# Token rows scattered back tile by tile, expert buffers of their own, and the split of the maxima moved off VectorE

## The chip, the cores and the metric

The kernel runs on one core of one Trainium2 chip, in float32 with some bf16 operands. The metric is the device time of one execution in microseconds (us), the median of several runs. A profile of one execution gives the rows quoted below.

## The reference

Two batches of tokens, each of 1024 rows with 128 features go through two layers. Layer 0 is a retention block (8 heads) and then a latent attention (16 heads of 8, causal) followed by a mixture of four experts, of which each row takes the best one. Layer 1 is a plain attention (16 heads of 8, with two masked corner scores) followed by a ternary linear layer. Cut to what the change touches:

```
logits = x @ gate_w.T + gate_b
top = argmax(logits, -1); onehot = one_hot(top, 4)
h = relu(einsum('btd,ehd->bteh', x, W1) + b1)
y = einsum('bteh,edh->bted', h, W2) + b2
moe = einsum('bted,bte->btd', y, onehot)

scores = where(causal, q @ k.T / sqrt(8), -inf)    # layer 1: no causal mask
attn = softmax(scores); out = (attn @ v) @ Wo.T
```

## The kernel before, in words

The retention comes first, then a short stage that makes queries and keys of the latent attention, and then one long stage, attention(), from some 350 us to the end, in which both attentions, the experts and the last layer are interleaved. All five engines walk through one list that order() (L855) returns; each engine takes from it the items that are its own.

**Units.** The scores are worked through in 32 blocks m (16 of the causal layer, m < BLOCKS, and 16 of layer 1). A block is four heads by 512 queries; its units are key tiles of 128: 4 or 8 per block in the causal layer, 8 in layer 1, 224 in all. Batch 0 of layer 0 is units 0 to 47, batch 1 48 to 95, batch 0 of layer 1 96 to 159, batch 1 of layer 1 160 to 223. The list counts in steps, and step s holds unit s: S (L1190, scores by TensorE), the exponentials by ScalarE (L1358), V (L1220, the product with the values, one unit behind), and one or two scans of a later unit.

**Maxima.** A scan is A (L1159): TensorE computes the scores of a later unit in another layout and VectorE reduces them to maxima (L1441). When a block is scanned, the item M turns 16 rows of 128 maxima into three bf16 parts of the negated maximum, which become extra rows of the queries, so that the softmax needs no subtraction. M is a transpose on TensorE (L1172), two operations on VectorE (L1454 and L1456), two on GpSimd (L1062 and L1063), and three small DMAs which GpSimd issues (L1070). The first S of the block waits for these DMAs. M comes 4 steps before that S in layer 1 (3 in its first block); in the causal layer it comes 3 steps before for blocks of 8 units and 7 for blocks of 4.

**PSUM ring.** Items that need a bank of their own (A, M, O, N, Y, H, G, C, x, h, y, D, k, q, v) share a ring of two places; TensorE fills a place once its reader, VectorE or ScalarE, has emptied it.

**Experts.** experts_of(b) (L834) puts the mixture of batch b into the list, from step z on (55 and 103). Rows are normed; TensorE makes the logits (G) and ranks (C); GpSimd scatters eight tiles of rows with indirect DMAs into an order by expert in DRAM (`sort`, L1083). Each expert's rows begin on a tile, so there are 11 tiles, some with rows that no token fills. SyncE loads them as one transfer (L981). x (L1280) transposes them, in three groups; h (L1295) and y (L1303) are the two products of a tile, with weights picked by a register. VectorE adds the bias and writes y over the row tile (L1546). The tiles come four to a step, from step z + 15 on.

**The way back.** store_rows (L997) on SyncE stores the results to DRAM in three groups. The item `back` on GpSimd (at step 73 for batch 0, and at step 120 for batch 1) waits for these three stores, gathers eight tiles of 128 rows in token order with indirect DMAs (L1093), and writes the constant columns of V again (L1097 and L1098), as the expert buffers of a batch lie in the space of its V. `sum` (L1104, step z + 22) adds them to the rows in two halves, `stat` on VectorE (L1552) takes the statistics of a half, `root` (L1110) is GpSimd's, `scale` (L1560) VectorE's over all eight tiles, and D, k, q, v (L1311, L1316, L1321) make the operands of layer 1. GpSimd's own items stand in one order, so an M that comes behind `back` waits for all of it.

**Weights of the experts.** w2 and b2 lie in the space of the query and key parts, so load_picks_of (L970) loads them for each batch.

## Time and profile before

| | |
|---|---|
| median of 3 runs | 1110.97 us (1110.78 to 1114.72) |
| profiled execution, its own time | 1113.98 us |
| its span | 1112.2 us |
| mean granted clock of TensorE | 0.921 |
| TensorE busy | 927.1 us (83%) |
| VectorE busy | 829.0 us (75%) |
| ScalarE busy | 650.0 us (58%) |
| GpSimd busy | 325.7 us (29%) |

Busy time is a mean over stages that differ: retention up to some 300 us, the causal layer and the experts of batch 0 up to some 650 us, layer 1 with the experts of batch 1 up to some 860 us, and the rest. The granted clock is a share of 2.4 GHz; 0.5 is 1.2 GHz. "Idle before" in square brackets is the time in which the engine had nothing running just before the instruction, with what ended it. TensorE's operand loads are PEld.

### The profile page before, as it was taken

How to read it: one execution, taken by the hardware profiler on the slowest of the kernel's cores; microseconds unless marked ns; L12 is line 12 of the kernel's file. 1: busy time of each engine (PE TensorE's matmuls, PEld its weight loads, DVE VectorE, ACT ScalarE, POOL GpSimd, SP SyncE). 2: the span in 40 equal slices, each digit the busy share in tenths (PEclk: the TensorE clock that was granted, in tenths of full speed). 3: DMA queues.
4: the chain of work that ended last, by engine and by line, in shares of the span. 5: the costliest groups of instructions: out<-in, count | busy, mean ns of one | idle time of the engine just before them, and what ended most of it. 6: DMA issues, size and time to landing. Idle time of an engine off the chain costs nothing.

```text
span 1112.2 us, 22861 instructions
## 1 busy us (share of the span) xinstructions
PE 927.1 (83%) x9022; PEld 479.3 (43%) x9022; DVE 829.0 (75%) x1377; ACT 650.0 (58%) x1311; POOL 325.7 (29%) x556
## 2 busy tenths in 40 slices
PE   5999999984675999989896678888969999999982
PEld 3777778774332344344382322336413223222231
DVE  3666667753857788887755658886778999999865
ACT  1555555453321677776634445865747888898860
POOL 2755566642232111102506200240431100100111
PEclk8999999996765899999998888999988999999995
DMA  7000000000041124301331232023204010000000
GB/s 269 1 2 1 1 1 2 1 1 6 1 154 46 35 75 130 88 24 35 102 87 28 81 108 78 21 58 94 80 4 164 19 35 18 20 18 2 5 20 19
DMA packets 50094, 53.79 MB, mean 48 GB/s; under 512 B 8635, under 2 KB 41147, under 8 KB 49701
## 3 DMA queue, kind: packets, MB, share of 16 engines
q1 hardware_dynamic: 45892, 49.79, 14.8%
q0 software_dynamic: 4096, 2.54, 0.9%
q8 instruction: 72, 1.18, 0.4%
q14 instruction: 34, 0.27, 0.1%
HBM read 33.66 MB, written 19.66 MB: 48 GB/s over the span
## 4 chain that ended last, share of the span: by engine, by line
PE 37%; DVE 26%; POOL 17%; issue 12%; ACT 6%; DMA 1%; SPq 0%; POOLq 0%; DVEq 0%; ACTq 0%
DVE arena L1441 16%; PE banks L1220 11%; PE banks L1190 7%; PE banks L1159 4%; ACT arena L1358 3%; POOL arena L711 2%; PE banks L1303 2%; PE banks L1295 2%; POOL arena L384 2%; POOL arena L710 2%; POOL arena L387 1%; POOL arena L714 1%; POOL arena L695 1%; POOL arena L1093 1%; PE banks L1198 1%
## 5 line engine op out<-in xcount | busy, mean ns | idle before, releaser
L1358 ACT ACTIVATE arena<-banks 128x512 f32<-128x512 f32 (+3 forms) x896 | 445.5, 552 | 181.0 <-PE banks L1198 86.5
L1441 DVE TENSOR_REDUCE arena<-banks 128x2 f32<-128x1024 f32 (+1 forms) x448 | 476.5, 1107 | 57.6 <-PE banks L1166 30.8
L1220 PE MATMUL banks<-arena 128*32 128x256 f32 (+1 forms) x3328 | 266.3, 393 | 10.3 <-ACT arena L1371 8.7
L1190 PE MATMUL banks<-arena 61*128 61x512 bf16 (+4 forms) x896 | 169.6, 374 | 36.4 <-ACT arena L1358 28.3
L1159 PE MATMUL banks<-arena 56*128 56x512 bf16 (+3 forms) x896 | 170.4, 376 | 28.0 <-DVE arena L1441 26.4
L1062 POOL CAST arena<-arena 16x128 bf16<-16x128 f32 x32 | 9.0, 281 | 441.4 <-DVE arena L1456 441.3
L1190 PEld LDWEIGHTS banks<-arena 61*128 61x128 bf16 (+1 forms) x896 | 44.3, 93 | 196.0 <-ACT arena L1358 164.5
L1220 PEld LDWEIGHTS banks<-arena 128*32 128x32 f32 x3328 | 67.2, 109 | 140.0 <-issue 78.9
L1159 PEld LDWEIGHTS banks<-arena 56*128 56x128 bf16 x896 | 45.4, 96 | 49.8 <-DVE arena L1441 45.1
L609 DVE TENSOR_REDUCE arena<-arena 128x8 f32<-128x1024 f32 x16 | 19.5, 1220 | 60.7 <-ACT arena L737 60.7
L734 ACT ACTIVATE arena<-banks 128x1024 f32<-128x1024 f32 x16 | 16.4, 1027 | 71.0 <-PE banks L584 69.3
L1070 POOL DMA_DIRECT2D arena<-arena x96 | 54.7, 574 | 10.7 <-POOL arena L1063 9.2
L748 ACT ACTIVATE arena<-banks,arena 128x128 f32<-128x128 f32 x128 | 46.4, 475 | 4.8 <-PE banks L593 4.8
L1166 PE MATMUL banks<-arena 64*128 64x128 bf16 x576 | 46.3, 232 | 0.0
L569 PE MATMUL banks<-arena 128*128 128x128 f32 x256 | 34.9, 292 | 7.9 <-DVE arena L641 7.9
L760 ACT ACTIVATE arena<-banks 128x1024 f32<-128x1024 f32 x16 | 16.4, 1027 | 37.7 <-PE banks L546 36.3
L1198 PE MATMUL banks<-arena 64*128 64x128 bf16 x512 | 37.4, 224 | 0.0
L569 PEld LDWEIGHTS banks<-arena 128*128 128x128 f32 x256 | 31.9, 202 | 10.6 <-DVE arena L641 8.5
L1166 PEld LDWEIGHTS banks<-arena 64*128 64x128 bf16 x576 | 30.0, 103 | 14.0 <-issue 4.4
L654 DVE TENSOR_TENSOR arena<-arena 128x1024 f32<-128x1024 f32 x16 | 32.9, 2059 | 3.0 <-POOL arena L387 3.0
L508 PE MATMUL banks<-arena 128*128 128x512 f32 x64 | 32.7, 634 | 2.1 <-DMA arena<-c_gk 2.1
L546 PE MATMUL banks<-arena 128*128 128x128 f32 x256 | 33.6, 286 | 0.2 <-DVE arena L623 0.2
(217 smaller groups left out, 1366.8 us busy)
## 6 DMA issues: line engine op xcount, KB each, us to landing
arena<-k_products SPq DMA_DIRECT2D x32, 224.0 KB
arena<-q_products SPq DMA_DIRECT2D x64, 112.0 KB
q_products<-arena SPq DMA_DIRECT2D x16, 384.0 KB, 3.4
k_products<-arena SPq DMA_DIRECT2D x16, 384.0 KB, 3.6
arena<-e_w SPq DMA_DIRECT2D x22, 256.0 KB, 3.8
arena<-e_w SPq DMA_DIRECT2D x2, 1024.0 KB, 6.6
arena<-arena POOLq DMA_DIRECT2D x96, 4.0 KB, 1.7
sorted_rows<-x SPq DMA_DIRECT2D x2, 704.0 KB, 8.6
```

The source lines that it names most:

```text
L546: ins = nc.tensor.matmul(bank(s // 4)[:, (s % 4) * P:(s % 4 + 1) * P], wg[:, s * P:(s + 1) * P], XT[:, i, :], start=True, stop=True)
L569: ins = nc.tensor.matmul(bank(7)[:, 0:P], uu[:, s, :], wo[:, s, :], start=(s == 0), stop=(s == RH - 1))
L654: v_.tensor_tensor(on, oc[i % 2], spread(grs, RH, P), ALU.mult).then_inc(o_normed, 1)
L748: ins = s_.activation(ga[:, s, :], bank(4 + s // 4)[:, (s % 4) * P:(s % 4 + 1) * P], ACT.Identity, scale=gn[:, 0, s:s + 1], bias=gn[:, 1, ...
L1070: g_.dma_start(rows, nmp[k % 2][:, i, :]).then_inc(mrow[k % 2], 16)
L1159: ins = nc.tensor.matmul(bank(first + par)[:, 0:hi - lo], Qs[k_][rows, qc, x, qo:qo + P], Ks[k_][rows, x, lo:hi], start=True, stop=not (di ...
L1166: ins = nc.tensor.matmul(bank(first + par)[:, o:o + P], masks[rows, one, :], masks[rows, two, :], start=False, stop=z == len(terms) - 1)
L1190: ins = nc.tensor.matmul(bank((q + par) % SCORES)[:, o:C], Ks[n % NS][rows, x, kt * P:(kt + 1) * P], Qs[n % NS][rows, c, x, o:C], start=Tr ...
L1198: ins = nc.tensor.matmul(bank((q + par) % SCORES)[:, o:o + P], masks[rows, 2 + z, :], masks[rows, z, :], start=False, stop=z == 1)
L1220: ins = nc.tensor.matmul(PS[h * VW:(h + 1) * VW, AV_BANK, o:end], V[:, b, kt, HG * g + h, :], Pr[u % PROBS][:, h, o:end], start=(kt == 0 a ...
L1358: s_.activation(Pr[s % PROBS][:, h, o:C], bank(q % SCORES)[:, o:C], ACT.Exp) \
L1441: v_.tensor_reduce(of, two_banks, AX.X, ALU.max).then_inc(ring_dve, 1)
```

## The change

1. **Scatter in place of gather.** Every sorted row carries its token number as a 129th column, so a row is 516 bytes. Rows that no token fills get numbers beyond the tokens (c_pads). A new item `put` (b, i), one step after y (b, i), scatters tile i with an indirect DMA to the token's place in DRAM. fetch_rows on SyncE waits for all 11 and loads the rows back with two plain transfers. store_rows and `back` are gone, and so is the writing of V's constant columns inside `back`.
2. **Space of their own** for xs, hsT, hid, hn, yg, b2 and w2, one set for both batches. b2 and w2 are loaded once.
3. **M** is read from PSUM by ScalarE (one operation, which copies with a factor of -1), and GpSimd makes all three parts (four operations). VectorE has no part in it.
4. **Batch 1's experts** come two tiles to a step over six steps in place of three, and `sum` comes at z + 26 in place of z + 22; what follows it moves with it.
5. **scale** is split in two halves one step apart; D of the first half waits only for its own.

```diff
+    pads = np.zeros((SORTED * P, P + 1), dtype=np.uint32)
+    pads[:, P] = T + np.arange(SORTED * P)
+    c["c_pads"] = pads.view(f)
+    c["c_token"] = np.arange(T, dtype=np.uint32).reshape(NT, P).T.copy().view(f)
...
-        xs_dram = [nc.dram_tensor(f"sorted_rows_{b}", [SORTED * P, P], F32, kind="Internal").ap() for b in range(B)]
-        ys_dram = [nc.dram_tensor(f"expert_rows_{b}", [SORTED * P, P], F32, kind="Internal").ap() for b in range(B)]
+        xs_dram = [nc.dram_tensor(f"sorted_rows_{b}", [SORTED * P, P + 1], F32, kind="Internal").ap() for b in range(B)]
+        ys_dram = [nc.dram_tensor(f"expert_rows_{b}", [T + SORTED * P, P], F32, kind="Internal").ap() for b in range(B)]
...
-        value_at = A.at
...
-        nm1 = A.tile(P, rows=MAXIMA)
+        nm1, nm2 = A.tile(P, rows=MAXIMA), A.tile(P, rows=MAXIMA)
...
+        xs, hsT, hid = A.tile(SORTED, P + 1), A.tile(SORTED * P), [A.tile(HID) for _ in range(2)]
+        hn = A.tile(NT, P + 1)
+        yg_at = A.at
+        h2T = A.tile(T)
+        A.at = yg_at
+        yg = A.tile(NT, P)
+        b2, w2, token = A.tile(NE * P), A.tile(NE * EM, P), A.tile(NT)
...
-        b2, w2 = A.tile(NE * P), A.tile(NE * EM, P)
...
-        xs, hsT, hid = [], [], []
-        for b in range(B):
-            A.at = value_at + b * NT * AH * VW
-            xs.append(A.tile(SORTED, P))
-            hsT.append(A.tile(SORTED * P))
-            hid.append([A.tile(HID) for _ in range(2)])
-            assert A.at <= value_at + (b + 1) * NT * AH * VW
...
-                sp.dma_start(xs_dram[b], d["x"][0:SORTED * P, :]).then_inc(xs_cleared, 16)
+                sp.dma_start(xs_dram[b], d["c_pads"]).then_inc(xs_cleared, 16)
...
-        BACK_AT = (18, 17)
...
+            pace, end = ((4, 22), (2, 26))[b]
...
-                  (14, ("x", (b, 0))), (14, ("x", (b, 1))), (15, ("x", (b, 2)))]
...
+            at += [(14 + g * 4 // pace, ("x", (b, g))) for g in range(len(GROUPS))]
             for i in range(SORTED + 1):
-                step = 15 + min(i, SORTED - 1) // 4
+                step = 15 + min(i, SORTED - 1) // pace
...
+                at += [(step + 1, ("put", (b, i - 1)))] * (i > 0)
...
-            at += [(BACK_AT[b], ("back", b)), (22, ("sum", b)), (23, ("stat", (b, 0))), (24, ("stat", (b, 1))),
-                   (24, ("root", b)), (25, ("scale", b)), (26, ("D", one)), (26, ("D", two)),
...
+            at += [(end, ("sum", b)), (end + 1, ("stat", (b, 0))), (end + 2, ("stat", (b, 1))), (end + 2, ("root", b))]
+            at += [(end + 3 + d, e) for d, e in (
+                (0, ("scale", one)), (1, ("scale", two)), (1, ("D", one)), (1, ("D", two)),
+                (1, ("k", one)), (1, ("q", one)), (1, ("k_part0", one)), (1, ("k_rem", one)), (1, ("q_part0", one)),
+                (2, ("k", two)), (2, ("q", two)), (2, ("q_rem", one)), (2, ("k_part1", one)), (2, ("k_part2", one)),
...
-        BY_ACT, BY_BOTH = "H x k".split(), "h"
+        BY_ACT, BY_BOTH = "M H x k".split(), "h"
...
-                    sp.dma_start(xs[b], xs_dram[b].rearrange("(i p) o -> p i o", p=P)).then_inc(xs_loaded[b], 16)
+                    if b:
+                        sp.wait_ge(ys_put[b - 1], 16 * SORTED)
+                    sp.dma_start(xs, xs_dram[b].rearrange("(i p) o -> p i o", p=P)).then_inc(xs_loaded[b], 16)
...
-                def store_rows(b, steer):
-                    back = ys_dram[b].rearrange("(i p) o -> p i o", p=P)
-                    for g in GROUPS:
-                        for i in g:
-                            if i + W1S < SORTED:
-                                load_w1(b, i + W1S, steer)
-                        t = slice(g[0], g[-1] + 1)
-                        taken(sp, "y", (b, g[-1]))
-                        sp.dma_start(back[:, t, :], xs[b][:, t, :]).then_inc(ys_stored[b], 16)
+                def fetch_rows(b):
+
+                    sp.wait_ge(ys_put[b], 16 * SORTED)
+                    sp.wait_ge(x_summed, 2 * b)
+                    rows = ys_dram[b][0:T].rearrange("(t p) o -> p t o", p=P)
+                    for c in range(2):
+                        t = slice(QT * c, QT * (c + 1))
+                        sp.dma_start(yg[:, t, :], rows[:, t, :]).then_inc(ys_back[c], 16)
...
-                    store_rows(b, steer)
+                    for i in range(W1S, SORTED):
+                        load_w1(b, i, steer)
...
+                for t, src in ((gate, d["e_gate"]), (enorm, d["k_norm"]), (w2, d["e_w2"])):
...
+                fetch_rows(0)
...
+                pool.wait_ge(load2, 160)
+                link(g_.tensor_copy(hn[:, :, P].bitcast(U32), token.bitcast(U32)))
...
-                        link(g_.tensor_copy(part[1], nm1))
-                        g_.tensor_tensor(part[2], nm1, part[1], ALU.subtract).then_inc(m_split, 1)
+                        ready(pool, mrow[k % 2], PARTS * 16 * (k // 2))
+                        link(g_.tensor_copy(part[0], nm1))
+                        link(g_.tensor_tensor(nm2, nm1, part[0], ALU.subtract))
+                        link(g_.tensor_copy(part[1], nm2))
+                        g_.tensor_tensor(part[2], nm2, part[1], ALU.subtract).then_inc(m_split, 1)
...
-                    elif kind == "back":
-
-                        pool.wait_ge(ys_stored[k], 16 * len(GROUPS))
-                        for t in range(NT):
-                            g_.indirect_dma_start(yg[:, t, :], None, ys_dram[k],
-                                                  bass.IndirectOffsetOnAxis(slot_i[:, t:t + 1], 0)) \
-                              .then_inc(ys_back[t // QT], 16)
-                        pads = V[:, k, :, :, AD:VW].rearrange("p t h e -> p (t h) e")
-                        g_.memset(pads[:, :, 0:1], 1.0)
-                        g_.memset(pads[:, :, 1:VW - AD], 0.0).then_inc(padded, 1)
+                    elif kind == "put":
+
+                        b, i = k
+                        taken(pool, "y", k)
+                        g_.indirect_dma_start(ys_dram[b], bass.IndirectOffsetOnAxis(xs[:, i, P:].bitcast(U32), 0),
+                                              xs[:, i, 0:P], None).then_inc(ys_put[b], 16)
...
-                            pool.wait_ge(ys_back[c], 16 * QT * (k + 1))
+                            pool.wait_ge(ys_back[c], 16 * (k + 1))
...
-                                    pe.wait_ge(padded, b + 2)
...
-                        pe.wait_ge(x1_ready, k // 2 + 1)
+                        pe.wait_ge(x1_ready, k + 1)
...
+                    elif kind == "M":
...
+                        ready(act, m_split, k)
+                        s_.activation(nm1, bank(ring_bank(r))[0:MAXIMA, 0:P], ACT.Copy, scale=-1.0).then_inc(ring_act, 1)
...
-                    elif kind == "M":
-
-                        ready(dve, mrow[k % 2], PARTS * 16 * (k // 2))
-                        row = bk[0:MAXIMA, 0:P]
-                        part = [nmp[k % 2][:, i, :] for i in range(PARTS)]
-                        link(v_.tensor_scalar(part[0], row, -1.0, None, ALU.mult))
-                        ready(dve, m_split, k)
-                        v_.scalar_tensor_tensor(out=nm1, in0=row, scalar=-1.0, in1=part[0],
-                                                op0=ALU.mult, op1=ALU.subtract).then_inc(ring_dve, 1)
...
-                        dve.wait_ge(x_rooted, k + 1)
-                        for i in range(k * NT, (k + 1) * NT):
+                        dve.wait_ge(x_rooted, k // 2 + 1)
+                        for i in range(k * QT, (k + 1) * QT):
```

## Rows read from the trace of the kernel before

**Rows 1.** Page, busy time and share of the span by engine.
```profile
PE 927.1 (83%) x9022; PEld 479.3 (43%) x9022; DVE 829.0 (75%) x1377; ACT 650.0 (58%) x1311; POOL 325.7 (29%) x556
```
**Rows 2.** Timeline, 589 to 610 us: start, length, engine, line, count, [idle before].
```profile
589.84 1.05 POOL L1093 DMA_INDIRECT arena<-expert_rows,arena  x1 [0.30 <-issue]
...
596.73 0.28 DVE L1456 SCALAR_TENSOR_TENSOR arena<-banks,arena 16x128 f32<-16x128 f32 x1
...
599.83 2.73 POOL L1098 MEMSET arena<- 128x2944 f32 x1
...
606.67 0.87 DVE L1552 BATCH_NORM_STATS2 arena<-arena 128x6 f32<-128x128 f32 x4 [8.22 <-POOL arena L1104]
...
609.11 1.12 PE L1228 MATMUL banks<-arena 128*128 128x128 f32 x4 [8.31 <-DVE arena L1441]
```
**Rows 3.** Windows of 3 us: busy PE, PEld, DVE, ACT, POOL, then clock, DMA.
```profile
609.00:612.00 3.00, 2.89 (x24) 1.56 (x24) 2.82 (x11) 0.92 (x2) 0.00 (x0) 0.50 0.00 0
...
810.00:813.00 3.00, 2.81 (x18) 0.64 (x22) 2.97 (x11) 0.62 (x2) 0.36 (x2) 0.53 0.00 0
```
**Rows 4.** Timeline, 806 to 811 us.
```profile
806.42 2.53 POOL L1104 TENSOR_TENSOR arena<-arena 128x512 f32<-128x512 f32 x2
807.58 0.39 PE L1190 MATMUL banks<-arena 61*128 61x512 bf16 x2 [2.28 <-DMA arena<-arena]
807.74 0.87 DVE L1552 BATCH_NORM_STATS2 arena<-arena 128x6 f32<-128x128 f32 x4 [3.95 <-POOL arena L1104]
...
810.19 0.61 PE L1159 MATMUL banks<-arena 56*128 56x512 bf16 x2 [2.22 <-DVE arena L1441]
```
**Rows 5.** Groups of VectorE by shape, 860 to 1040 us: count, busy, mean ns, idle before.
```profile
L1456 DVE SCALAR_TENSOR_TENSOR arena<-banks,arena 16x128 f32<-16x128 f32 x9 | 2.5, 280 | 0.3
L1454 DVE TENSOR_SCALAR arena<-banks 16x128 bf16<-16x128 f32 x9 | 2.4, 268 | 0.0
```
**Rows 6.** Windows of 20 us: experts of batch 1, then last stage.
```profile
760.00:780.00 20.00, 18.09 (x158) 14.85 (x160) 9.95 (x27) 8.49 (x23) 0.00 (x0) 1.00 0.42 104
...
880.00:900.00 20.00, 19.07 (x205) 5.18 (x201) 19.46 (x22) 17.68 (x35) 2.36 (x5) 1.00 0.09 25
```
**Rows 7.** Who waited for whom, 860 to 1000 us: total, times, longest.
```profile
PE banks L1159 <- DVE arena L1441: 3.5, 7, 0.5
```
**Rows 8.** Timeline of one M, 904 to 907 us.
```profile
904.08 0.28 PE L1172 MATMUL banks<-arena 128*16 128x128 f32 x1
...
904.77 1.09 ACT L1358 ACTIVATE arena<-banks 128x512 f32<-128x512 f32 x2 [0.29 <-PE banks L1190]
...
905.69 0.28 POOL L1062 CAST arena<-arena 16x128 bf16<-16x128 f32 x1 [17.32 <-DVE arena L1456]
906.05 0.40 POOL L1063 TENSOR_TENSOR arena<-arena 16x128 bf16<-16x128 f32 x1
```
**Rows 9.** Line L1190, what ended TensorE's idle time before it: total, times.
```profile
  DMA arena<-arena: 17.1, 14
```
**Rows 10.** Groups of ScalarE by shape, whole trace.
```profile
L1358 ACT ACTIVATE arena<-banks 128x128 f32<-128x128 f32 x64 | 14.3, 276 | 12.9 <-PE banks L1198 12.9
```
**Rows 11.** Line L1083, then L981: issue to landing.
```profile
DMA to landing us min/median/max: 2.2/2.9/4.7
...
DMA to landing us min/median/max: 5.0/5.6/6.2
```
**Rows 12.** DMA issues by line: KB each, median us to landing.
```profile
expert_rows<-arena SPq DMA_DIRECT2D x4, 256.0 KB, 2.5
```
**Rows 13.** Timeline: load of the sorted rows (SyncE's queue) and first transpose.
```profile
543.31 0.38 SPq L981 DMA_DIRECT2D arena<-sorted_rows  x1
...
550.67 0.66 PE L1280 MATMUL banks<-arena 128*128 128x128 f32 x4
...
749.67 0.38 SPq L981 DMA_DIRECT2D arena<-sorted_rows  x1
...
755.53 0.66 PE L1280 MATMUL banks<-arena 128*128 128x128 f32 x4
```

More of the change, by code:

```diff
@@ L786, in build @@
         xs_loaded = [sem(f"sorted_loaded_{b}") for b in range(B)]
-        ys_stored = [sem(f"expert_rows_stored_{b}") for b in range(B)]
+        ys_put = [sem(f"expert_rows_put_{b}") for b in range(B)]
         ys_back = [sem(f"expert_rows_back_{h}") for h in range(2)]
@@ new lines, in experts_of @@
+            at += [(end, ("sum", b)), (end + 1, ("stat", (b, 0))), (end + 2, ("stat", (b, 1))), (end + 2, ("root", b))]
[3 more added lines that the diff above has]
+                (2, ("k", two)), (2, ("q", two)), (2, ("q_rem", one)), (2, ("k_part1", one)), (2, ("k_part2", one)),
+                (2, ("q_part1", one)), (2, ("q_part2", one)), (2, ("k_part0", two)), (2, ("k_rem", two)),
+                (3, ("q_part0", two)), (3, ("q_rem", two)), (3, ("k_part1", two)), (3, ("k_part2", two)),
+                (3, ("q_part1", two)), (3, ("q_part2", two)), (4, ("v", one)), (5, ("v", two)))]
@@ L1044, in _ @@
                 load_all(11)
+                fetch_rows(1)
                 store_parts(1, 1)
@@ L1076, in _ @@
                         link(root_of(g_, link, xrr[:, t], xss[:, t], newt[:, 0, t]))
-                        g_.tensor_tensor(hn, U[:, t, :], spread(xrr[:, t], NT, P), ALU.mult).then_inc(e_normed, 1)
+                        g_.tensor_tensor(hn[:, :, 0:P], U[:, t, :], spread(xrr[:, t], NT, P), ALU.mult) \
+                          .then_inc(e_normed, 1)
                     elif kind == "sort":
@@ L1279, in _ @@
                         for o, i in enumerate(GROUPS[g]):
-                            ins = nc.tensor.transpose(bk[:, o * P:(o + 1) * P], xs[b][:, i, :], ident)
+                            ins = nc.tensor.transpose(bk[:, o * P:(o + 1) * P], xs[:, i, 0:P], ident)
                         ins.then_inc(ring_full, 1)
@@ L1381, in _ @@
                         act.wait_ge(u_squared, 4 * b + q + 1)
+                    elif kind == "M":
+                        r = place[kind, k]
+                        act.wait_ge(ring_full, r + 1)
+                        ready(act, m_split, k)
+                        s_.activation(nm1, bank(ring_bank(r))[0:MAXIMA, 0:P], ACT.Copy, scale=-1.0).then_inc(ring_act, 1)
                     elif kind == "H":
```

50 lines of the change are left out of this document (17 added, 33 removed).

## The prediction

> **What bounds the kernel now.** I read the busy shares first [rows 1]: TensorE 83%, VectorE 75%, ScalarE 58%, so no engine bounds the whole and stages must be told apart. I went next to the chain of waits and the windows. Three things stand out.
>
> In the last stage VectorE and TensorE are almost level: in 20 us VectorE is busy 19.46 and TensorE 19.07 at the full clock, ScalarE 17.68 [rows 6]. TensorE waits for it, but never longer than 0.5 us, once or so for each block [rows 7], in the place where VectorE works on M. So VectorE bounds, with TensorE half a microsecond per block behind.
>
> Where the experts' rows come back there is a stall in each batch. In batch 0 GpSimd gathers eight tiles from 589.84 on, writes constant columns for 2.73 us, does the M that stands behind, and sums. VectorE waits 8.22 us for the sum and TensorE 8.31 us for VectorE [rows 2]. In batch 1 VectorE waits 3.95 us, TensorE 2.28 us for the maxima rows that GpSimd sends late, and then 2.22 us for VectorE [rows 4]. After each, TensorE runs at the half clock (1.2 GHz) for a while [rows 3].
>
> While the expert products run, TensorE is busy 18.09 of 20 us, VectorE 9.95 [rows 6]: TensorE bounds there.
>
> **Part by part.** All in the frame of the profiled execution, 1113.98 us.
>
> *The way back of batch 0.* M of step 73 ends on GpSimd 0.30 ahead of the first gather, at 589.5 [rows 2], and now 0.55 later (below), at 590.1. Seven tiles have been put by then, beside TensorE's products, when GpSimd has nothing else. Four puts stand behind that M. A put should cost what the scatters and gathers do: 0.94 to 1.05 us and 0.30 of issue, 1.26 together [rows 2], so they end at 595.1. Landing after the last is 2.9 us by the median, 2.2 to 4.7 [rows 11]: 598.0. SyncE issues a plain transfer (0.38 [rows 13]); its landing I put at 2.5 us, as a store of the same 256 KB has [rows 12], so the first half is there at 600.9. GpSimd meanwhile does the M of step 77, whose maxima leave VectorE at 597.0 [rows 2], until 600.6. The first half of the sum takes 1.26 (half of 2.53 [rows 4]): 602.2 in place of 606.67 [rows 2]. Gain 4.5; I take 4.0. It can't be over 8.2, VectorE's whole wait. Low end: a landing of 4.7 and a slow fetch of 4 us leave 1; and if the puts queue up, nothing.
>
> *The way back of batch 1.* The last tile is put at step 124 and the sum stands at step 129: some five units of 2.5 us, 12 us, against the same 2.9 + 0.4 + 2.5 us. No one waits. The M of step 124 is no longer behind gathers. VectorE's 3.95 us and most of TensorE's 4.5 go; they are largely the same time, so 4.0. Bounds 0 and 4.5.
>
> *The half clock behind the two stalls.* 609 to 612 us has 2.89 us of TensorE work at 0.50, and 810 to 813 has 2.81 at 0.53 [rows 3]. At full clock half of each would be saved, 1.4 and 1.4. For batch 0 some idle time stays, so 1.0; for batch 1 1.2. Together 2.2, bounds 0 and 2.8.
>
> *M off VectorE.* Each M frees 0.268 + 0.280 us [rows 5] and a gap, 0.57. Only where VectorE bounds is it time: the blocks of layer 1, 15 M in the scans behind 670 us. There TensorE follows by 0.5 us at most [rows 7]. With some lost to TensorE's own floor I take 0.37 each: 15 x 0.37 = 5.5. Bounds 0 (TensorE takes over at once) and 15 x 0.57 = 8.6. In the causal layer VectorE has slack, so 0 there. ScalarE's operation: the nearest row is the exponential of 128 x 128 from PSUM, 0.276 us [rows 10]. ScalarE stands idle for 0.29 us at this very point, between M's transpose at 904.08 and the next exponential at 904.77 [rows 8], so the 0.28 fits into that idle time. Behind it are the next exponentials, for which S and V wait. 0.03 us each, 1.0 in all; if ScalarE had no cover, 32 x 0.28 = 9.0.
>
> *The chain of M gets longer.* Before: two operations of VectorE, then 0.28 and 0.40 on GpSimd, 1.4 us to the DMAs. After: 0.28 on ScalarE, then 0.28 + 0.40 + 0.28 + 0.40 with gaps of 0.08 on GpSimd [rows 8], 1.95 us. That is 0.55 more before the three DMAs. It costs only where S waits for the rows: 17.1 us of weight load and matmul idle in 14 records [rows 9], of which I count, by the waits of each stretch, three cases of 1 to 2 us (near 373, 651, 685), the one of batch 1 which goes, and five of 0.2 to 0.6, each in a causal block with 3 steps of lead. 3 x 0.55 + 5 x 0.4 = 3.6; I take 3.5. Bounds 0 and 32 x 0.55 = 17.6.
>
> *Sorted rows of 516 bytes.* The load of the sorted rows is issued at 543.31 and takes up to 6.2 us [rows 11, 13]; the first transpose is at 550.67 [rows 13], so the slack in batch 0 is 1.2 us. In batch 1 it is 0.8: issued at 749.67, landed 5.0 us later, used at 755.53 [rows 11, 13]. A scatter and a load a little slower eat this up: 1.0 in all. Bounds 0, and if the load took twice its 5.6 us, 2 x (5.6 - 1.0) = 9.
>
> *Two tiles per step.* The products are bound by TensorE [rows 6], whose work is the same, spread beside six units in place of three. VectorE bounds the three other units by little: 0.3 gained. Halved `scale`: 0 (1.1 us moved behind the reductions of the next step; TensorE's transposes waited for those anyway), bounds -1 and +1. w2 and b2 loaded once: 1.3 MB less beside the stacks near 669 us, 0.5 gained, since the maxima DMAs of one block (wait of 1 us at 685) are near it. SyncE's order changes little: fetch_rows(0) stands where the last store stood, ahead of store_parts, which waits for much later work. GpSimd's token copy and one more load at the start are beside idle time: 0.
>
> **Sum.** -4.0 - 4.0 - 2.2 - 5.5 + 1.0 + 3.5 + 1.0 - 0.3 - 0.5 = -11.0. The profiled execution would take 1103.0. It was 3.0 above the median of the runs (1110.97), so the median becomes 1100.0.
>
> **Rivals.**
>
> 1. *TensorE takes over at once in the last stage*, so that the freed 0.57 us is no time: -5.5 goes away, 1105.5. For it: 19.07 of 20 us busy [rows 6]. Against it: the 0.5 us waits [rows 7]. 17%.
>
> 2. *Batch 0 gains nothing*: the way back is as long as it was, since scatter, landing in DRAM, SyncE and fetch are four hand-overs in a row where two were. The 4.0 and its 1.0 of clock go: 1105. For it: landings up to 4.7 [rows 11]. Against: 3 us of constant columns and half of the issues go in any case. 12%.
>
> 3. *The removed stalls give back more.* Later in the same stage TensorE falls to the half clock again, as ScalarE and VectorE hand each other small items; if these run denser, some 5 us more are gained: 1095. For it: granted clock 0.921 over the span. Against it: these later waits have causes of their own, which the change leaves. 13%.
>
> 4. *Slower: the chain of M decides.* Place: the four or five engines between the last reduction and the S of each of the 32 blocks. If ScalarE reads M late, because exponentials stand ahead of it, each M costs 0.55 + 0.28 = 0.83 us on the path: 26.6 us in place of the 4.5 in the sum, so 11 us slower than before, 1122. The point from which it decides is 15.5 us over 32 blocks, 0.48 us per block. For it: S already waits for the rows in eight blocks [rows 9]. Against it: most of these waits are under 0.6 us, and blocks of layer 1 have a step more of lead. 8%.
>
> 5. *The change does not do what it says*: the puts are slow (eleven in place of eight, 13.9 us of GpSimd in place of 10), delay M and the sum, and eat what the rest gives: 1111. 5%.
>
> **Chances and range.** The forecast has 45%, the rivals 17, 12, 13, 8 and 5. A change under 0.5%, 5.6 us, can't be told from none here; that is 1105.4 to 1116.5. Rivals 1 and 2 stand just at that border, so I split their 29% evenly: faster 45 + 13 + 14.5, same 14.5 + 5, rounded to 0.73, 0.19 and slower 0.08. Forecast, rivals 1 to 3 and half of rival 5 lie within 1091 to 1111, more than 8 in 10. The forecast's own range is 1096 to 1104.
>
> **What would show it.** VectorE's wait before the statistics of batch 0 should be 3 to 5 us in place of 8.22, and that of batch 1 gone. The windows right behind should show the full clock in batch 1. In the last stage a block should take 0.3 to 0.5 us less, VectorE and TensorE both near 19.4 of 20. Waits of L1190 for the maxima rows should grow by about 0.5 us each near 373, 651 and 685, and be no more than ten. The load of the sorted rows should land in 5.5 to 8 us. The prediction is wrong if waits for the maxima rows show in every block, if ScalarE's operation on M holds up exponentials, or if the first sum of batch 0 starts later than 603.

## The result and the profile after

The changed kernel takes 1122.07 us (median of 6 runs, 1119.28 to 1126.24), the kernel before on the same chip 1112.85 us (6 runs). The ratio is 1.0087, with a 95% interval of 1.0055 to 1.0119. It is slower, where 11 us less were forecast. The profiled execution took 1119.28 us, its span 1117.5 us: 5.3 us more than before. All figures of the traces below are in the frame of these two. Medians and ratios leave out two executions in a second, slower state of the chip: one of e9 (4357 us) and one of the kernel before in the fifth set (1205 us).

The busy shares of the changed kernel, from its page, as in [rows 1]:

```profile
PE 936.1 (84%) x9022; PEld 482.6 (43%) x9022; DVE 814.1 (73%) x1313; ACT 657.4 (59%) x1343; POOL 348.1 (31%) x623
```

VectorE lost 15 us of work, as intended. TensorE has the same 9022 matmuls and needs 9 us more for them: it ran at the half clock for longer. This points to new waits.

M is transposed once for each of the 32 blocks, so the start of that matmul (L1172 in both kernels) is a clock to compare them by. Blocks are counted from 0:

| start of M's transpose, us | before | after | after is later by |
|---|---|---|---|
| block 2 | 379.0 | 380.0 | 1.0 |
| block 11 | 527.2 | 538.5 | 11.3 |
| block 14 | 595.7 | 611.7 | 16.0 |
| block 15 (behind the way back of batch 0) | 643.7 | 652.9 | 9.2 |
| block 20 | 797.6 | 806.7 | 9.1 |
| block 22 (behind the way back of batch 1) | 864.0 | 867.6 | 3.6 |
| block 31 | 1047.3 | 1051.2 | 3.9 |
| end of the span | 1112.2 | 1117.5 | 5.3 |

So the ways back gave what was hoped (6.8 and 5.5 us), the last stage gave nothing, and the causal layer lost more than that. The step from block 1 to block 2, ahead of the table, is part of it: 11.8 us before, 14.1 after.

**The causal layer.** Its stretch from M of block 2 to M of block 11, in two windows (length, then busy PE, PEld, DVE, ACT, POOL, then clock, DMA share, GB/s). Before:

```profile
379.00:527.00 148.00, 134.03 (x1897) 62.05 (x1893) 119.25 (x174) 106.40 (x252) 25.79 (x52) 0.99 0.24 69
```

After:

```profile
380.00:538.50 158.50, 139.25 (x1898) 62.55 (x1894) 115.41 (x156) 109.02 (x261) 31.92 (x70) 0.95 0.22 65
```

The same matmuls (1897 and 1898 records) take 5.2 us longer, TensorE is idle for another 5.3 us, and the granted clock falls from 0.99 to 0.95. Line L1190 (S, the scores) says why. What ended TensorE's idle time before it, as in [rows 9]:

```profile
  DMA arena<-arena: 33.8, 18
```

It was 17.1 in 14 [rows 9]. Both count a wait of the weight load and the same wait of its matmul; of the matmul alone it was 7.3 us in 5 cases and is 15.7 in 9. Now one such case closely, the M of block 3, whose transpose starts at 398.74 before and at 399.74 after. First the timeline of before:

```profile
400.08 0.40 POOL L1063 TENSOR_TENSOR arena<-arena 16x128 bf16<-16x128 f32 x1
...
400.77 1.68 POOL L1070 DMA_DIRECT2D arena<-arena  x3 [0.29 <-POOL arena L1063]
...
402.31 0.75 SPq L961 DMA_DIRECT2D arena<-k_products  x2
...
403.62 0.39 PE L1190 MATMUL banks<-arena 59*128 59x512 bf16 x2
```

And of after:

```profile
400.06 0.27 ACT L1386 ACTIVATE arena<-banks 16x128 f32<-16x128 f32 x1
...
401.58 0.40 POOL L1066 TENSOR_TENSOR arena<-arena 16x128 bf16<-16x128 f32 x1
...
402.27 1.67 POOL L1073 DMA_DIRECT2D arena<-arena  x3 [0.29 <-POOL arena L1066]
...
403.32 1.06 SPq L957 DMA_DIRECT2D arena<-k_products  x2
...
406.73 0.61 PE L1190 MATMUL banks<-arena 59*128 59x512 bf16 x2 [2.08 <-DMA arena<-arena]
...
407.43 1.09 ACT L1357 ACTIVATE arena<-banks 128x512 f32<-128x512 f32 x2 [3.76 <-PE banks L1190]
```

From M's transpose to the first of the three maxima DMAs it was 2.03 us and is 2.53 us: 0.5 us more, as forecast. But TensorE now waits 2.08 us where its matmul waited not at all, and the matmul behind the wait takes 0.61 us in place of 0.39, which is the level of 1.2 GHz (the granted clock from 406.7 to 412.7 is 0.50; before it was 1.00 from 403.6 to 406.6). Look at the order of two issues. SyncE starts the loads of the next stack (two of 224 KB here) when enough units of the running block have their scores. Before, GpSimd issued the last maxima DMA (4 KB) at 401.9, ahead of that load at 402.31; now at 403.4, behind it at 403.32, and from 404 to 406 us, while S waits, the DMA engines are busy for 0.66 and then 0.88 of the time. The landings of the three DMAs, first before, then after:

```profile
DMA to landing us min/median/max: 1.7/1.7/2.1
```

```profile
DMA to landing us min/median/max: 1.7/2.0/3.3
```

The last of the three landed after 1.7 us before (issued at 401.9, and S starts at 403.62); now it lands after 3.3 (403.4, and S starts at 406.73). So 0.5 us of chain became 0.5 + 1.6 us, which are the 2.1 us by which S starts later behind M's transpose. There was no slack: before, the weight load of this S already waited 0.2 us for the same DMA. The Trainium skill says in "DMA: Bandwidth & Descriptors", section "Queues, rings and completion order", that each DMA engine goes round its queues and takes a whole packet of one before it turns to the next; if so, a small transfer can pay for a large one on another queue. The two landings fit this; that it happens packet by packet no run here shows.

**The way back of batch 0**, the timeline of after, to be read against [rows 2]:

```profile
609.92 0.94 SPq L999 DMA_DIRECT2D arena<-expert_rows  x2
...
616.00 2.15 POOL L1104 TENSOR_TENSOR arena<-arena 128x512 f32<-128x512 f32 x2
...
617.14 0.87 DVE L1548 BATCH_NORM_STATS2 arena<-arena 128x6 f32<-128x128 f32 x4 [2.77 <-POOL arena L1104]
...
619.59 0.66 PE L1227 MATMUL banks<-arena 128*128 128x128 f32 x4 [2.86 <-DVE arena L1446]
```

VectorE waits 2.77 us in place of 8.22, TensorE 2.86 in place of 8.31. From the transpose of block 14's M to the start of the sum it is 4.3 us (611.67 to 616.00), where it was 9.6 (595.74 to 605.3). In batch 1 neither waits for the sum (from M of block 20 to that of block 22: 66.4 us before, 60.9 after).

**The last stage.** The window of after beside the second of [rows 6], and the wait of [rows 7]:

```profile
880.00:900.00 20.00, 19.08 (x213) 5.40 (x205) 19.00 (x20) 17.78 (x35) 3.04 (x7) 1.00 0.09 26
```

```profile
PE banks L1159 <- DVE arena L1446: 3.5, 7, 0.5
```

VectorE is busy for 19.00 of 20 us in place of 19.46, and a block still takes 20.0 us. TensorE's wait is what it was, 3.5 us in 7 cases. The timeline of one M, beside [rows 8]:

```profile
907.97 0.27 ACT L1386 ACTIVATE arena<-banks 16x128 f32<-16x128 f32 x1
...
908.35 1.09 ACT L1357 ACTIVATE arena<-banks 128x512 f32<-128x512 f32 x2
...
908.75 0.39 PE L1159 MATMUL banks<-arena 56*128 56x512 bf16 x2 [0.50 <-DVE arena L1446]
...
909.19 2.36 DVE L1446 TENSOR_REDUCE arena<-banks 128x2 f32<-128x1024 f32 x2 [0.49 <-PE banks L1159]
```

And VectorE and TensorE at the M of before, which [rows 8] leave out:

```profile
905.04 0.27 DVE L1454 TENSOR_SCALAR arena<-banks 16x128 bf16<-16x128 f32 x1
...
905.18 0.39 PE L1159 MATMUL banks<-arena 56*128 56x512 bf16 x2 [0.50 <-DVE arena L1441]
905.34 0.28 DVE L1456 SCALAR_TENSOR_TENSOR arena<-banks,arena 16x128 f32<-16x128 f32 x1
...
905.61 2.36 DVE L1441 TENSOR_REDUCE arena<-banks 128x2 f32<-128x1024 f32 x2
```

ScalarE's M fits into its idle time. TensorE's wait of 0.50 us is there with M and without it, and from the start of its scores to the next reduction it is 0.43 us before and 0.44 after. VectorE stands idle for 0.49 us just where its M was: TensorE may write the next maxima scores only when the reduction before M has emptied their place of the ring, and VectorE has nothing to reduce until they are there. M used to fill this gap.

### The profile page after: what moved, and what is told of

Same layout as the page of the kernel before. It is cut to its first block, busy times and chain, and to the rows that moved or that the text cites. A ratio compares the mean times of both kernels' runs of the same rounds, so it can differ in the third digit from the quotient of the medians.

```text
span 1117.5 us, 22892 instructions
## 1 busy us (share of the span) xinstructions
PE 936.1 (84%) x9022; PEld 482.6 (43%) x9022; DVE 814.1 (73%) x1313; ACT 657.4 (59%) x1343; POOL 348.1 (31%) x623
## 4 chain that ended last, share of the span: by engine, by line
PE 37%; DVE 25%; POOL 16%; issue 12%; ACT 6%; DMA 3%; SPq 0%; POOLq 0%; DVEq 0%; ACTq 0%
DVE arena L1446 16%; PE banks L1219 11%; PE banks L1190 8%; PE banks L1159 5%; ACT arena L1357 4%; DMA arena<-arena 3%; POOL arena L705 2%; PE banks L1294 2%; POOL arena L377 2%; PE banks L1302 2%; POOL arena L704 2%; POOL arena L380 1%; POOL arena L708 1%; POOL arena L689 1%; POOL arena L379 1%
## 5 line engine op out<-in xcount | busy, mean ns | idle before, releaser
L1219 PE MATMUL banks<-arena 128*32 128x256 f32 (+1 forms) x3328 | 269.3, 397 | 8.2 <-ACT arena L1370 6.6
L1190 PE MATMUL banks<-arena 61*128 61x512 bf16 (+4 forms) x896 | 171.9, 379 | 44.1 <-ACT arena L1357 27.5
L1190 PEld LDWEIGHTS banks<-arena 61*128 61x128 bf16 (+1 forms) x896 | 44.5, 93 | 205.2 <-ACT arena L1357 166.3
L563 PE MATMUL banks<-arena 128*128 128x128 f32 x256 | 36.1, 299 | 7.9 <-DVE arena L635 7.9
L1097 POOL DMA_INDIRECT expert_rows<-arena x22 | 21.6, 980 | 49.9 <-DVE arena L1542 48.0
```

Of the source, the lines that this page charges most:

```text
L563: ins = nc.tensor.matmul(bank(7)[:, 0:P], uu[:, s, :], wo[:, s, :], start=(s == 0), stop=(s == RH - 1))
L1190: ins = nc.tensor.matmul(bank((q + par) % SCORES)[:, o:C], Ks[n % NS][rows, x, kt * P:(kt + 1) * P], Qs[n % NS][rows, c, x, o:C], start=Tr ...
L1219: ins = nc.tensor.matmul(PS[h * VW:(h + 1) * VW, AV_BANK, o:end], V[:, b, kt, HG * g + h, :], Pr[u % PROBS][:, h, o:end], start=(kt == 0 a ...
```

## The experiments

The runs come in five sets. Kernels of one set ran on one chip beside the kernel before; on two of the chips that took about 1130 us and on the others 1112 to 1114, so each ratio is against the kernel before of its own set, and medians are compared within a set.

**First set: which blocks' M costs.** The kernel before took 1130.42 us. Theory A in all that follows: the longer chain of M lets its last DMA collide with the stack load in the causal layer. The others are its rivals, each told in the expectation that names it.

The edit of e1, e2 and e3 gives M back to VectorE in some blocks of the changed kernel, with GpSimd's two-operation split:

```diff
+        def by_vector(k):
+            return True            # e1;  e2: k < BLOCKS;  e3: k >= BLOCKS
-                    elif kind == "M":            (ScalarE)
+                    elif kind == "M" and not by_vector(k):
+                    elif kind == "M" and by_vector(k):            (VectorE)
+                        link(v_.tensor_scalar(part[0], row, -1.0, None, ALU.mult))
+                        v_.scalar_tensor_tensor(out=nm1, in0=row, scalar=-1.0, in1=part[0], ...)
```

e4 is the kernel before with the changed kernel's M and nothing else of the change.

> The changed kernel with M as it was (two operations on VectorE, two on GpSimd) in all 32 blocks. Theory A (the longer chain of M costs the causal layer some 12 us, since its DMAs now meet the stack loads; the ways back gained 4 and 5.5 us as forecast; M off VectorE gained nothing in layer 1): 1101 to 1106, some 8 us faster than the kernel before, and S waits for maxima rows as short as before. Theory B (M off VectorE gains in layer 1 and the loss is in the new way back or the buffers): 1122 or slower.

Measured: 1114.33 us, ratio 0.9866 (0.9844 to 0.9888). The stretch from block 2 to 11 takes 147.7 us again.

> The changed kernel with M as it was in the 16 causal blocks alone; ScalarE and GpSimd make M in layer 1. Theory A: the same as with M as it was everywhere, 1101 to 1107. Theory B: faster than that by 5 us if VectorE's time counts in layer 1. Rival C (the layer 1 blocks lose too, by the longer chain): slower than it by 2 us or more.

Measured: 1118.97 us, 0.9900 (0.9877 to 0.9923); the stretch 147.6 us.

> The changed kernel with M as it was in the 16 blocks of layer 1 alone. Theory A: like the changed kernel, 1119 to 1125, as the loss is in the causal blocks and VectorE's two operations in layer 1 fill a gap in which it would wait for TensorE anyway. Theory B: 5 us slower than the changed kernel. Rival C: 2 us or more faster than it.

Measured: 1131.75 us, 1.0008 (0.9991 to 1.0024); the stretch 159.8 us.

> The kernel before with nothing changed but M (ScalarE reads, GpSimd splits, four operations). Theory A: 1121 to 1127, some 11 us slower than before, with S waits of about 2 us before blocks 1, 3, 5 and 7. Theory B: faster than before by up to 5 us.

Measured: 1145.73 us, 1.0125 (1.0095 to 1.0154); the stretch 160.1 us. The new M alone costs the kernel before 15.3 us, more than the 11 expected. It lies in the causal layer: e3, which has it there, is 17.4 us above e1.

e2, which has it in layer 1, is 4.6 us above e1 (their intervals just overlap), but its profile puts little of this into layer 1: from M of block 15 to that of block 31 it takes 402.5 us and e1 401.5. The rest lies ahead of block 2, where the two kernels are the same: S waits 2.77 us there for the maxima of block 1 in e2, 0.85 in e1. This one wait differs between profiles with the same M, from 0.6 to 2.8 us, and its cause is open: e11, below, waits 2.33 us there for a maxima DMA that landed after 3.4 us, though SyncE issues no load there between 350 and 373.5 us. So in layer 1 the new M shows no gain of 5.5 us, and at most a small loss.

**Second set: collision or ScalarE.** The kernel before took 1130.34 us. The changed kernel again, as control:

> The changed kernel once more, on the chip of the runs beside it. All theories: slower than before by 0.5 to 1.2%, as in its first timing; S waits of about 2 us before blocks 1, 3, 5 and 7.

Measured: 1133.93 us, 1.0015 (0.9995 to 1.0034); the stretch 160.3 us. Nearer to the kernel before than in the first timing and outside the 0.5 to 1.2% expected; more on this below. The waits of S before blocks 3, 5 and 7 are there, 2.36, 2.10 and 2.26 us.

e5 and e6 leave M as it is and move only the stack loads of the causal layer:

```diff
-                        at = LOAD_AT.get(n, (0, 8) if l else (4, 7))
+                        at = LOAD_AT.get(n, (0, 8) if l else (5, 8))        # e6: (3, 6)
```

> The changed kernel with the paced stack loads of the causal layer let go one unit later (5 and 8 in place of 4 and 7). Theory A with the mechanism named (the later M DMAs now share the DMA engines with the stack load that the first S's predecessor lets go): the S waits before blocks 3, 5 and 7 fall from 2.1 to under 0.8 us, the last maxima DMA lands in under 2.2 us, and the kernel is 6 to 12 us faster than the changed one. Rival D (the chain is simply too long, the stack loads have no part in it): waits and time stay.

Measured: 1124.82 us, 0.9936 (0.9911 to 0.9960); the stretch 151.0 us. The same place in the timeline of e5:

```profile
403.10 1.67 POOL L1073 DMA_DIRECT2D arena<-arena  x3 [0.29 <-POOL arena L1066]
...
405.95 0.39 PE L1190 MATMUL banks<-arena 59*128 59x512 bf16 x2 [0.48 <-DMA arena<-arena]
...
407.68 0.31 SPq L957 DMA_DIRECT2D arena<-k_products  x1
```

The load now starts at 407.68, long after the maxima are there. Of the wait of 2.1 us, 0.48 is left: the 0.5 of the chain itself, which is what was forecast. The other 1.6 is the collision. But e5 gains 9.1 us, and M costs more than that: on chips of 1130 us e1 stands at 0.9866 and e5 at 0.9936, some 8 us apart. Part of the rest is seen: 0.48 us before each of blocks 3, 5 and 7, and 2.63 us before block 1. That one is not this collision: SyncE issues no load between 362 and 376.5 us in e5. No run takes the rest apart.

> The changed kernel with the stack loads of the causal layer let go one unit earlier (3 and 6). Theory A: the loads still run while the M DMAs are issued, so waits of 1.5 to 3 us stay, and the time is within 4 us of the changed kernel. Rival D: the same time. A fall of the waits would say that only a load which starts in the last microsecond matters.

Measured: 1129.53 us, 0.9997 (0.9976 to 1.0018), 4.4 us below the changed kernel; the stretch 155.6 us, waits of 1.4 to 1.7 us. This fits loads that still overlap with the maxima DMAs, only less.

e7 puts the half microsecond into the kernel before, without ScalarE:

```diff
                         link(g_.tensor_copy(part[1], nm1))
+                        if k < BLOCKS:
+                            link(g_.tensor_tensor(nm2, nm1, part[1], ALU.subtract))
```

> The kernel before, M on VectorE and GpSimd as it was, with one more operation of 0.4 us on GpSimd (its result isn't used) in each of the 16 causal blocks. Theory A (0.5 us of chain is all it takes): S waits of 1.5 to 2.3 us before blocks 3, 5 and 7, and 7 to 13 us slower than before. Rival E (what costs is that ScalarE reads M, behind and ahead of exponentials): within 2 us of before.

Measured: 1149.41 us, 1.0154 (1.0124 to 1.0184); the stretch 161.6 us. The timeline of e7 at block 3:

```profile
404.46 0.40 POOL L1064 TENSOR_TENSOR arena<-arena 16x128 f32<-16x128 f32 x1
404.94 0.40 POOL L1065 TENSOR_TENSOR arena<-arena 16x128 bf16<-16x128 f32 x1
405.63 1.68 POOL L1072 DMA_DIRECT2D arena<-arena  x3 [0.29 <-POOL arena L1065]
...
406.70 0.75 SPq L961 DMA_DIRECT2D arena<-k_products  x2
...
409.96 0.61 PE L1192 MATMUL banks<-arena 59*128 59x512 bf16 x2 [1.93 <-DMA arena<-arena]
```

The last maxima DMA is issued at 406.8, again just behind the load. One idle operation of 0.4 us in 16 blocks, 6.4 us of an engine that is busy for 29% of the time, costs 19 us, more than the 7 to 13 expected. Theory A stands, and ScalarE isn't needed for the loss.

**Third set: the rest of the change, and a better version.** The kernel before took 1111.94 us.

> The kernel before once more, with a profile, beside the others of this call: the control for e4 and e7 and for the ratio of the changed kernel (1.0087 in the first timing, 1.0015 in the second). Theory P (place): the kernel before has on these chips, beside what its first trace shows, stalls of about 6 us each that no semaphore explains, near 540 us and twice near 780 to 830 us, where the changed kernel has one less; then its span is 1125 to 1132 us, and the stretch from the second M to the twelfth stays at 148 us, with no wait of S over 0.6 us in it after block 1. Theory Q: its causal layer suffers there as that of the changed kernel does; the stretch is then over 153 us.

Measured: 1107.69 us in its one run, the stretch 147.0 us. This chip is one of those at 1112 us and had none of the extra stalls, so theories P and Q can't be told apart by it.

e8 is e1 with e5's loads. It has all of the change but M.

> Changed kernel with M as before (VectorE and two operations of GpSimd) and the causal stack loads paced (5, 8) in place of (4, 7). Theory A (the collision of the last maxima DMA with the stack load is all there is in the causal layer, and with the short chain there is none): the later loads have nothing left to repair, so the time is that of M as before alone, 1114 +- 2 us where the kernel before takes 1130. Rival: moving the loads is worth something by itself (2.5 us or more, as the wait before block 1 and the loads' own traffic shrink): 1111 or less.

Measured: 1104.11 us, 0.9916 (0.9892 to 0.9941). The times that were expected are those of a chip at 1130 us, and e1 was not run on one at 1112; so what the later loads are worth by themselves rests on e10.

> The kernel before with only the causal stack loads paced (5, 8) in place of (4, 7): the control for e5. Theory A: the kernel before has no collision to repair, ratio 0.998 to 1.002 against itself. Rival: the later loads help whatever the chain of M is; then it gains what the changed kernel gained, some 6 to 9 us, ratio 0.992 to 0.995.

Measured: 1113.58 us, 1.0012 (0.9994 to 1.0030). The later loads gain nothing in the kernel before, so what e5 gained comes from the collision. And e8 against e10, which differ by all of the change but M: 9.5 us less. The forecast for these parts (its sum without the terms of M) was 10.0.

e9 takes back two tiles per step in batch 1:

```diff
-            pace, end = ((4, 22), (2, 26))[b]
+            pace, end = ((4, 22), (4, 22))[b]
```

> Changed kernel with M as before, and batch 1 in steps of four tiles with its sum at step 22, as in batch 0 (two tiles per step and step 26 undone). If two tiles per step are worth what was forecast (0.3 us): 1115 beside 1114.3 of M as before alone, same within 2 us. Rival: the spread is what empties the way back of batch 1, and four units less are left for it now; then VectorE waits 3 to 5 us for the sum of batch 1 as it does in batch 0, and the time is 1118 to 1120.

Measured: 1107.49 us (median of four runs; the 1108.87 named further down is that of all five), 0.9946 (0.9904 to 0.9987). VectorE did not wait for the sum, against the rival; from block 20 to 22 it took 63.3 us, and 57.6 in e8.

**Fourth set: layer 1, and the size of M's cost.** The kernel before took 1113.64 us.

> The changed kernel a third time, beside the changed kernel with M as before and the stack loads later on the same chip. So far it stood at 1.0087 and at 1.0015 against the kernel before, on two chips. Theory A: M costs it 14 to 20 us wherever it runs, so it is 1.3 to 1.8% above the kernel with M as before; against the kernel before the ratio is 1.005 to 1.010 where that takes about 1112 us, and near 1.001 where that takes about 1130. Rival: the first ratio was the chip's, and M costs under 10 us here.

Measured: 1119.78 us, 1.0051 (1.0031 to 1.0071).

> Changed kernel with M as before and the causal stack loads paced (5, 8), a second time, as the base for the three others. Ratio to the kernel before 0.989 to 0.994 where that takes about 1112 us, 0.984 to 0.988 where it takes about 1130.

Measured: 1102.75 us, 0.9891 (0.9869 to 0.9914). The changed kernel is 17.0 us above it: the price of its M with the loads where they were. Their profiles are 22.3 us apart: 5.5 lie between blocks 1 and 2, 11.9 between blocks 2 and 11, 3.2 from there to block 15, and 0.7 between blocks 15 and 31.

e11 adds work to VectorE in layer 1, e12 takes it away there. Both start from e8; e12 uses `k < BLOCKS` as e2 does.

```diff
+                        for _ in range(2 if k >= BLOCKS else 0):
+                            link(v_.tensor_scalar(nm2, row, -1.0, None, ALU.mult))
                         link(v_.tensor_scalar(part[0], row, -1.0, None, ALU.mult))
```

> The kernel of e8 with two operations more of VectorE ahead of M in the 16 blocks of layer 1 (0.27 us each, results unused). It measures what VectorE's time is worth there. Theory C (VectorE's M fills a gap in which the ring's two places make it wait anyway, and no more than that gap): what is added now has no gap, so a block takes 20.5 us in place of 20.0 and the kernel 7 to 9 us more, though the same 0.55 us taken away gave nothing. Rival (TensorE bounds, and VectorE has slack of its own): the period stays 20.0 to 20.1 and the kernel takes under 2 us more.

Measured: 1104.77 us, 0.9917 (0.9896 to 0.9939), 2.0 us above e8 in the same set.

> The kernel of e8 with M by ScalarE and the longer split in the blocks of layer 1 alone. M off VectorE where VectorE is the fullest engine, with the causal layer untouched. Theory C: the freed 0.57 us turns into VectorE's wait for TensorE's next scores, period 20.0 us, 0 to 2 us more in all (the longer chain costs a little before the first block of layer 1 and at batch 1). Rival, the forecast on record: 0.37 us less per block, 5 us less in all.

Measured: 1104.19 us, 0.9928 (0.9900 to 0.9956), 1.4 us above e8, with intervals that overlap. The window of 20 us in the last stage, in e8, then e11, then e12:

```profile
960.00:980.00 20.00, 19.07 (x199) 5.07 (x197) 19.51 (x22) 17.78 (x34) 2.35 (x5) 1.00 0.01 2
```

```profile
960.00:980.00 20.00, 19.07 (x205) 5.68 (x197) 19.79 (x24) 17.73 (x34) 2.28 (x6) 1.00 0.09 25
```

```profile
960.00:980.00 20.00, 19.07 (x199) 5.06 (x197) 19.06 (x20) 17.93 (x35) 3.04 (x7) 1.00 0.09 24
```

From e12 through e8 to e11 VectorE's busy time goes from 19.06 through 19.51 to 19.79 of 20 us, and TensorE stays at 19.07. From block 24 to block 31 e12 took 143.5 us, e8 143.2 and e11 144.4. Taking 0.55 us of VectorE's M away saves nothing, and adding as much costs 0.16 us per block as a mean. It is not spread evenly: e11 is 0.55 and 0.44 us longer in the two blocks of 21.6 us (24 and 25) and 0.12 us in the five behind them together, which take 20 us. So half of my theory C fell: the gap at M is real, but in most blocks more than the gap is free. That the period is then TensorE's with its hand-overs is likely from this, and not shown by a run that shortens TensorE's work.

**Fifth set: the spread.** The kernel before took 1113.07 us. e14 is e9's edit on e8, e13 spreads batch 0 too, `((2, 26), (2, 26))[b]`.

> The kernel of e8 with batch 1 not spread (four tiles per step, sum at step 22), to settle a term: e9, the same with the old pacing of the stacks, took 1108.87 us with an interval of 0.4%, where e8 took 1104.11. Theory S: the spread is worth about 5 us, since all the units before the projections of batch 1 then have some product beside them, and TensorE works on at the full clock; 1107 to 1110 where e8 takes 1103 to 1104, ratio about 0.996. Rival (two tiles per step worth 0.3 us as forecast): within 1.5 us of e8, ratio 0.990 to 0.993.

Measured: 1105.19 us, 0.9913 (0.9882 to 0.9943), where e8 had 0.9916 and 0.9891. From block 20 to 22 it took 62.9 us. The profiles say that the spread is worth 5 us in that stretch, the times of whole runs say 0 to 3. The 0.3 of the forecast isn't refuted.

> The kernel of e8 with batch 0 spread too: two tiles per step and the sum at step 26, as in batch 1. In e8 batch 1 loses nothing at the way back and batch 0 still has a wait of VectorE of 2.6 us for its sum and one of TensorE of 2.7 us. Theory S (four units more between the last put and the sum hide the way back): the wait of VectorE before the statistics of batch 0 goes, and the kernel takes 2 to 4 us less than e8, some 1100 where the kernel before takes 1113. Rival: the projections of layer 1 now come four units later and have no such units to run beside, so its first stacks are late; 0 to 6 us more than e8.

Measured: 1106.40 us, 0.9932 (0.9904 to 0.9959). From its timeline:

```profile
646.16 0.78 SPq L963 DMA_DIRECT2D arena<-k_products  x2
...
648.81 0.78 SPq L963 DMA_DIRECT2D arena<-k_products  x2
...
651.52 1.04 PE L1169 MATMUL banks<-arena 56*128 56x512 bf16 x4 [9.19 <-DMA arena<-q_products]
```

The wait of VectorE for the sum of batch 0 is gone, as theory S said, and TensorE then waits 9.19 us for layer 1's first stack, as its rival said: the units that hid the way back are missing behind it. e8 remains the best, 0.8% to 1.1% below the kernel before and 1.5% below the changed one.

## Why the prediction was wrong

The step that failed is the cost of the longer chain of M. The prediction put it at 3.5 us, as "three cases of 1 to 2 us" that grow by 0.55 and five that grow by 0.4, "each in a causal block". It measured 15 to 17 us, just inside the bound of 17.6 that the prediction gave: e4 has 15.3 alone, the changed kernel stands 17.0 above e8, and e7 has 19 for 0.4 us in the causal blocks. Of the mechanism I had the place and the half microsecond right, and counted it as a pure delay. I did not ask what the three DMAs would collide with half a microsecond later, though SyncE's load of the next stack stood 0.4 us behind the last of them in the trace of before. The wait is then 2.1 us and not 0.5, ScalarE runs dry for 3.8 us, and TensorE falls to 1.2 GHz behind it. In blocks 3, 5 and 7 TensorE's matmul had no wait at all before, and the prediction counted waits that were there already. Moving the loads away (e5) takes back 9.1 us; the rest, some 6 to 8, is not traced to single causes, and the wait before block 1 within it is not this collision.

The second step is M off VectorE, put at 5.5 us gained, measured 0: e12 is 1.4 us above e8, no clear difference, and the block stays at 20.0 us. Rival 1 said so, at 17%. I took a wait of TensorE for VectorE as a proof that VectorE bounds. It was the wait for the ring's place, which ends with the reduction ahead of M; M ran beside that wait and beside the scores that followed, and was hidden.

The other terms held as a sum, 9.5 us by e8 and e10 where 10.0 was forecast, though not each by itself:

- *Way back of batch 0*, 4.0 and 1.0 of clock. M of block 14 to M of block 15: 45.9 us in e10, 41.1 in e8 the second time, 4.8 less (47.9 and 41.2, 6.7 less, in the two first profiles). VectorE's wait fell to 2.77 us, below the 3 to 5 forecast.
- *Way back of batch 1*, 4.0 and 1.2, with 0.3 of the spread: block 20 to 22 took 66.4, 64.6 and 67.3 us in three profiles of the old way on chips at 1112 us (63.6 and 63.8 in e4 and e7 on the others), 63 with the new way and no spread, 57.6 to 61.4 with it. So the way back gave some 1 to 4, less than forecast, and 0.3 was low for the spread by the profiles, which give 1.5 to 5.7.
- *Puts* cost 0.98 us, landed after 2.3 us by the median (forecast 2.9); the fetch landed after 3.2 us (forecast 2.5). The fetch of the first half was issued at 609.92 and no landing took over 3.5 us; the sum began at 616.00, right when GpSimd had issued M's DMAs (614.19 to 615.99). So what held it in the end was M ahead of it in GpSimd's order, not the rows.
- *ScalarE's operation* 0.27 us (forecast 0.28), in idle time, where 1.0 was put on it.
- *Sorted rows of 516 bytes* landed after 5.2 us by the median of two loads (4.7 and 5.8), 5.6 before [rows 11], and no transpose waited for them; 1.0 was put on it. The 30% that the prediction estimated from the Trainium skill's "DMA: Bandwidth & Descriptors", section "How a descriptor splits into AXI transactions", isn't borne out here.
- *The halves of `scale`*, w2 and b2 have no run of their own; no cost of theirs stands out in the traces.

Rival 4, the slower case, gave 1122 us, which is the median measured, but by another sum: 0.83 us in each of 32 blocks. That the numbers meet is luck. It was two operations' worth of delay in four or five blocks of the causal layer that decided, at up to four times its own size, and most of the other blocks pay nothing or 0.5. At 8% it was priced too low, because its price had no collision in it.

What stays open: the ratio of the changed kernel was 1.0087, 1.0015 and 1.0051 on three chips. Where the kernel before took 1130 us the traces have stalls of 4 to 6 us that no semaphore of the kernel explains, as this one in e1:

```profile
539.12 0.60 ACT L1380 ACTIVATE arena<-banks 128x512 f32<-128x512 f32 x1 [5.41 <-remote]
```

The kernels built on the one before show one more of them late in the run: ScalarE has two of 6.1 to 6.2 us between 740 and 840 us in e4 and e7, and one of 5.9 to 6.4 in e1, e3, e5 and the changed kernel. From M of block 15 to that of block 20 it takes 152 to 154 us with either kernel on the chips at 1112 us, and on the others 168 in e4 and e7 against 157 to 159. This would explain the ratio of 1.0015, but there is no profile of the kernel before itself on such a chip.

The traces do show where the large ones stand: at the end of GpSimd's runs of eight indirect DMAs. The one above follows the scatters of `sort` in batch 0, the common late one those of batch 1. The extra one follows the gathers of `back`, which the change took away; from e4:

```profile
827.41 0.94 POOL L1096 DMA_INDIRECT arena<-expert_rows,arena  x1 [0.30 <-issue]
...
830.16 1.09 ACT L1361 ACTIVATE arena<-banks 128x512 f32<-128x512 f32 x2 [6.15 <-remote]
```

The same gathers and scatters on the chips at 1112 us leave no such stall. Why they do on two chips is not known.

## What to carry to other kernels

When a step ahead of a small DMA gets longer, look in the trace at what other queues start in the next microsecond: the delay is then not what was added but what it collides with, here four times as much, with the half clock on top. Moving the large load away took one line here and gave back about half; leaving the step short gave back all. And an engine that waits for another at a ring's place does not show that the other is the bound: ask whether the work to be removed stands ahead of the release or behind it.

## What the chip showed that was not expected

A DMA of 4 KB issued 0.1 us behind a load of 224 KB on another queue landed after 3.3 us; issued 0.4 us ahead of it, it landed after 1.7. A slow landing can also come without such a load: at block 1 of e11 a maxima DMA landed after 3.4 us while SyncE issued nothing. An idle operation of 0.4 us on an engine busy 29% of the time cost 19 us in 16 blocks. VectorE busy for 19.8 of 20 us was still hardly the bound: 0.55 us more of its work cost 0.16 us per block, and almost nothing in five blocks of seven.
